# Adapters in fp16 halves, turned by DMA, in a four-layer conditioned residual kernel

## The reference

```
x = x + attention16(x, f)                 # 16 heads of 32; K, V from x and f, Q from f; @ Wo + bo
x = x + softmax((x + embed[stage]) @ f.T) @ f
x = x + layernorm(x + relu(x @ W1 + b1) @ W2 + b2) * gamma + beta      # W1: 512x128, by language
x = x + (x @ lora_A.T) @ lora_B.T + lang_embed                         # rank 16, by language
```

## Time and profile before

| what | value |
|---|---|
| median of 3 runs | 1295.74 us (1295.46 to 1296.12) |
| the profiled execution | 1295.73 us, span 1294.0 us |
| busy: PE, PEld | 1257.0 us (97%), 523.5 us (40%) |
| busy: DVE, ACT, POOL | 864.2 us (67%), 847.8 us (66%), 490.0 us (38%) |
| mean granted PE clock | 0.991 |

### The profile page before, as it was taken

How to read it: one execution, slowest core, us unless ns; L and a number is a source line. 1 busy time by engine, 2 the same in 40 slices (tenths; PEclk the granted TensorE clock), 3 DMA queues, 4 the chain that set the end, 5 groups by cost and what they waited for, 6 DMA issues and landing times.

```text
span 1294.0 us, 19231 instructions
## 1 busy us (share of the span) xinstructions
PE 1257.0 (97%) x6697; PEld 523.5 (40%) x6697; DVE 864.2 (67%) x1561; ACT 847.8 (66%) x1795; POOL 490.0 (38%) x428
## 2 busy tenths in 40 slices
PE   7999999999999999999999999999999999999996
PEld 4332454325543354433544245442454324543243
DVE  6886459764697538975389743987449855597544
ACT  5887359863598536975379742888339873598631
POOL 6604353233631246331552416514344143532024
PEclk9999999999999999999999999999999999999996
DMA  6303522225224153142421333213432136222020
GB/s 217 83 6 107 124 57 66 79 80 99 52 63 122 37 98 68 47 125 63 86 58 50 117 79 77 58 50 108 98 75 66 46 95 124 50 66 90 4 33 33
DMA packets 156142, 98.85 MB, mean 76 GB/s; under 512 B 107338, under 2 KB 130182, under 8 KB 156046
## 3 DMA queue, kind: packets, MB, share of 16 engines
q1 hardware_dynamic: 155984, 97.61, 30.9%
q10 hardware_dynamic: 62, 0.01, 0.0%
HBM read 40.81 MB, written 8.40 MB: 38 GB/s over the span
## 4 chain that ended last, share of the span: by engine, by line
PE 69%; DVE 15%; ACT 12%; issue 2%; POOL 1%; DMA 1%; SPq 0%; ACTq 0%; POOLq 0%; DVEq 0%
PE bank L478 25%; PE banks L478 13%; PE banks L1443 8%; DVE nmx L1095 8%; PE bank L1459 7%; ACT banks L816 5%; PE banks L1378 4%; ACT big L867 4%; PE bank L1280 3%; PE bank L1406 2%; PE bank L1411 2%; PE bank L1433 2%; PE bank L1469 1%; DVE y L1053 1%; ACT bank L896 1%
## 5 line engine op out<-in xcount | busy, mean ns | idle before, releaser
L816 ACT ACTIVATE banks<-banks,nmx 128x512 f32<-128x512 f32 x512 | 341.2, 682 | 40.2 <-DVE nmx L1095 37.8
L1095 DVE TENSOR_REDUCE nmx<-banks 128x1 f32<-128x512 f32 x512 | 329.2, 687 | 19.5 <-PE banks L1378 18.6
L867 ACT ACTIVATE big<-banks 128x1024 f32<-128x1024 f32 x256 | 248.0, 1021 | 54.4 <-PE banks L1443 53.4
L478 PE MATMUL bank<-fT,w_hi 128*128 128x512 f16 x768 | 255.7, 379 | 0.6 <-DVE fT L1009 0.6
L1378 PE MATMUL banks<-KQ 97*128 97x512 f16 x512 | 195.6, 382 | 8.1 <-ACT banks L816 7.9
L513 POOL TENSOR_TENSOR split<-tiles_in,ones 128x512 f16<-128x512 f32 x56 | 62.0, 1108 | 224.7 <-DMA xT<-split 205.7
L1443 PE MATMUL banks<-KQ 98*128 98x512 f16 x512 | 143.5, 383 | 3.6 <-DVE q L1116 0.2
L478 PE MATMUL bank<-fT,w_lo 128*128 128x512 f16 x384 | 145.4, 379 | 0.0
L513 POOL TENSOR_TENSOR half<-qk,ones 128x512 f16<-128x512 f32 x64 | 68.4, 1069 | 200.6 <-ACT qk L798 192.5
L1459 PE MATMUL bank<-big,V 128*32 128x512 f32 x1024 | 136.4, 605 | 0.0
L588 POOL TENSOR_TENSOR x<-x,bo_rows 128x512 f32<-128x512 f32 x32 | 39.9, 1275 | 206.5 <-DMA x<-in_x_dram 206.5
(11 more groups left out here) (154 smaller groups left out, 1822.0 us busy)
## 6 DMA issues: line engine op xcount, KB each, us to landing
KQ<-half SPq DMA_DIRECT2D x384, 64.0 KB, 2.0
tiles_in<-in_x_dram SPq DMA_DIRECT2D x32, 256.0 KB, 7.7
x<-in_x_dram SPq DMA_DIRECT2D x8, 1024.0 KB, 5.7
out_dram<-x SPq DMA_DIRECT2D x32, 256.0 KB, 2.0
tiles_in<-in_fside_BxSxS_dram SPq DMA_DIRECT2D x28, 256.0 KB, 3.8
w<-in_L_cond_W_dram SPq DMA_DIRECT2D x16, 256.0 KB, 4.5
b2r<-in_L_cond_b_dram SPq DMA_DIRECT2D x8, 256.0 KB, 4.3
gr<-in_L_cond_gamma_dram SPq DMA_DIRECT2D x8, 256.0 KB, 5.5
```

Of the source, the lines that this page charges most:

```text
L478: mm = eng.matmul(out_ap, pairs[n][0], pairs[n][1], start=(first and n == 0), stop=(last and n == len(pairs) - 1))
L816: eng.activation(bank(step, i)[:, v, :], bank(step, i)[:, v, :], ACT.Exp, bias=nmx[:, t, h:h + 1], accum_out=esum[:, t, h:h + 1]).then_inc ...
L867: eng.activation(big[:, n % 2, 2 * u:2 * u + 2, :], bank(step)[:, :, :], ACT.Exp).then_inc(read(step), 1)
L1095: eng.tensor_reduce(nmx[:, t, h:h + 1], bank(step, i)[:, v, :], AX_X, ALU.max, negate=True).then_inc(max_done, 1)
```

## The change

In all batches but the last the adapters' turns leave PE. `X2` (at the head of the middle stage) splits x into an fp16 high half (ACT) and a low half (VectorE, right behind each PV1 addition) in p16, and SP turns each tile by DMA into aT2. `X3` splits the normed x on GpSimd, and `T3` has SP turn it. In the last batch PE still turns, and high and low halves are taken by ACT and VectorE behind it. w1, lora_A and lora_B are held as fp16 halves: HID is made by `hi_lo` with 256 columns for two tiles at once, LOW by 16 f16 matmuls of 256 columns, LORA by one f16 matmul a tile. ADP stays fp32. The norm is rewritten: `U` takes (y - mean) * gamma on VectorE before the root is known, Newton is 11 operations of fused form over all four tiles (over two in the last batch), and SCALE is one VectorE operation. The addition of beta is moved ahead. The list of the middle stage is new, and SP turns tile 0 of f earlier.

```diff
+        at = {3: [("HID", 0)], 5: [("ADP", 0)], 6: [("ADP", 1), ("SQ", 0)], 7: [("HID", 1), ("SQ", 1)], 8: [("U", 0)],
+              9: [("ADP", 2), ("U", 1)], 10: [("ADP", 3), ("SQ", 2)], 11: [("SQ", 3), ("U", 2)], 12: [("NORM", 0), ("U", 3)],
+              13: [("SCALE", 0), ("SCALE", 1)], 14: [("X3", 0), ("SCALE", 2), ("SCALE", 3)], 15: [("X3", 1)],
+              16: [("X3", 2), ("T3", 0)], 17: [("X3", 3), ("T3", 1)], 19: [("T3", 2)], 20: [("T3", 3)],
+              24: [("LOW", 0)], 25: [("LORA", 0)], 27: [("LORA", 1)], 29: [("LOW", 1)], 31: [("LORA", 2)], 33: [("LORA", 3)]}
+        adapters = [at.get(n, []) for n in range(max(at) + 1)]
...
+    out, later = [("X2", t) for t in range(NT) if tail], {}
...
# GpSimd
+                    elif step[0] in ("X2", "X2T"):
...
+                        eng.tensor_tensor(yb[:, t, :], x1[:, t, :], b2r[:, :], ALU.add).then_inc(xb_done, 1)
+                        if head and t == NT - 1:
+                            add_beta(range(NT), head, i)
...
+                    elif step[0] == "X3":
                         t = step[1]
-                        eng.wait_ge(normed, i * NT + t + 1)
-                        eng.tensor_tensor(y[:, t % 2, :], y[:, t % 2, :], gr[:, :], ALU.mult).then_inc(scaled, 1)
-                        eng.wait_ge(scaled, i * NT + t + 1)
-                        eng.wait_ge(xg_done, i * NT + t + 1)
-                        eng.tensor_tensor(x1[:, t, :], y[:, t % 2, :], x1[:, t, :], ALU.add).then_inc(x3_done, 1)
+                        eng.wait_ge(x3_done, i * NT + t + 1)
+                        eng.wait_ge(x2t_in[t // 2], i * 32 + 32)
+                        split(p16[:, t, 0:S], p16[:, t, S:2 * S], x1[:, t, :], x3_hi, i * NT + t + 1, x3_lo)
# SP
+                    elif step[0] == "T3":
+                        t = step[1]
+                        eng.wait_ge(x3_lo, i * NT + t + 1)
+                        turn(aT2, t, p16[:, t, :], x3t_in[t // 2])
...
                 for t in range(NT):
+                    if head and t == NT - 1:
+                        wait_full(eng, ("S1", NT - 1), i)
+                        turn_f(0, b)
                     wait_read(eng, ("S1", t), i)
                     eng.dma_start_transpose(p1T[:, t, :, :, :].rearrange("p h k n -> p (h k) n"), p16[:, t, :]
                                             ).then_inc(p1t_in[t], 16)
                 if head:
-                    for n in range(NT):
-                        eng.wait_ge(f_lo, b * NT + n + 1)
-                        turn(fT, n, b, ft_in)
+                    turn_f(1, b)
+                    for t in range(NT):
+                        if t == NT // 2:
+                            turn_f(2, b)
+                            turn_f(3, b)
+                        eng.wait_ge(x2_lo, i * NT + t + 1)
+                        turn(aT2, t, p16[:, t, :], x2t_in[t // 2])
# VectorE
+            def norms_of(n, head, i):
+                tiles = NT if head else NT // 2
...
+                eng.wait_ge(sq_done, i * NT + at.stop)
+                eng.tensor_scalar(var, st[:, at, 2], 1.0 / D, EPS, ALU.mult, ALU.add).then_inc(newton, 1)
+                eng.wait_ge(newton, base + 1)
+                eng.tensor_scalar(r_int, si[:, at, 3], -0.5, 0x5F3759DF, ALU.mult, ALU.add).then_inc(newton, 1)
+                for k in range(base + 2, base + NEWTON, 3):
+                    eng.wait_ge(newton, k)
+                    eng.scalar_tensor_tensor(out=c, in0=var, scalar=-0.5, in1=r, op0=ALU.mult, op1=ALU.mult).then_inc(newton, 1)
...
+            def centre(t, i):
+                eng.wait_ge(sq_done, i * NT + t + 1)
+                eng.scalar_tensor_tensor(out=yb[:, t, :], in0=yb[:, t, :], scalar=st[:, t, 1:2], in1=gr[:, :],
+                                         op0=ALU.add, op1=ALU.mult).then_inc(normed, 1)
+            def scale(t, head, i):
...
+                eng.scalar_tensor_tensor(out=x1[:, t, :], in0=yb[:, t, :], scalar=st[:, t, 4:5], in1=x1[:, t, :],
+                                         op0=ALU.mult, op1=ALU.add).then_inc(x3_done, 1)
...
+                        if head:
+                            eng.wait_ge(x2_hi, i * NT + t + 1)
+                            eng.scalar_tensor_tensor(out=p16[:, t, S:2 * S], in0=x1[:, t, :], scalar=1.0, in1=p16[:, t, 0:S],
+                                                     op0=ALU.mult, op1=ALU.subtract).then_inc(x2_lo, 1)
# PE
                     elif kind == "LOW":
+                        at = tokens(step, head)
+                        if head:
+                            eng.wait_ge(x3t_in[step[1]], i * 32 + 32)
...
+                        for d in range(ND):
+                            for h in range(2):
+                                rows = a16[:, h, d, :, :].rearrange("p c r -> p (c r)")
+                                mm = eng.matmul(bank(step, i)[0:3 * LR, 0:at.stop - at.start], rows, aT2[:, h, d, at],
+                                                start=(d == h == 0), stop=(d == ND - 1 and h == 1))
```

More of the change, by code:

```diff
@@ L122, in order_mid @@
         if adapters and i % 2 == 0:
-            out += [a for a in (adapters.pop(0),) if a]
+            out += adapters.pop(0)
         if rows and not sums and i >= late and not adapters:
@@ L134, in order_mid @@
     assert rows and i >= max(later)
-    return out + [a for a in adapters if a] + ([] if sums else [("SROW",)])
+    return out + [a for each in adapters for a in each] + ([] if sums else [("SROW",)])
 OPEN = ((32, 26, 26, 26), (24, 24, 24, 24))
@@ L210, in order_last, with tokens @@
             + [("X2T", 0), ("HID", 0), ("X2T", 1), ("PV1", 2), ("ADP", 0), ("HID", 1), ("SQ", 0),
[L211 to L214, removed]
+               ("PV1", 3), ("ADP", 1), ("U", 0), ("SQ", 1), ("X2T", 2), ("U", 1), ("NORM", 0),
+               ("HID", 2), ("X2T", 3), ("SCALE", 0), ("HID", 3), ("X3T", 0), ("SCALE", 1), ("ADP", 2), ("LOW", 0),
+               ("X3T", 1), ("SQ", 2), ("ADP", 3), ("LOW", 1), ("U", 2), ("SQ", 3), ("U", 3), ("NORM", 1),
+               ("LORA", 0), ("LORA", 1), ("SCALE", 2), ("X3T", 2), ("SCALE", 3), ("LOW", 2), ("X3T", 3),
                ("LORA", 2), ("LOW", 3), ("LORA", 3)])
-ADAPTER_STEPS = set(order_mid(True, False))
+ADAPTERS = ("X2", "X2T", "HID", "ADP", "SQ", "U", "NORM", "SCALE", "X3", "T3", "X3T", "LOW", "LORA")
+def tokens(step, head):
+    n = NT // 2 if head else 1
+    return slice(step[1] * n * P, (step[1] + 1) * n * P)
 def plan_banks():
@@ L598, in _ @@
             add_bo(B - 1)
[L599 removed]
+            split_w1(B - 1)
+            mid(True, False, B - 1, [step for step in order_last() if step[0] in ADAPTERS])
         @block.sync
@@ L870, in attention @@
                 wait_full(eng, ("PREPB",), i)
[L871 to L873 removed]
+                eng.activation(lowB[0:LOW_ROWS, :], lone[2][0:LOW_ROWS, :], ACT.Copy, scale=WS).then_inc(b_hi, 1)
             def layer1(i, head, order=ORDER_L1):
@@ L1197, in attention @@
                     take_norms(g, i)
-                for g in range(1, NG):
+                finish_group(1, i)
+                small_columns(i)
+                for g in range(2, NG):
                     finish_group(g, i)
+                eng.wait_ge(b_hi, i + 1)
+                low = slice(2 * LR, 3 * LR)
+                eng.scalar_tensor_tensor(out=lowB[low, :], in0=lone[2][low, :], scalar=WS, in1=lowB[low, :],
+                                         op0=ALU.mult, op1=ALU.subtract).then_inc(read(("PREPB",)), 1)
             def layer1(i, head, order=ORDER_L1):
@@ L1480, in small_tables @@
                 mm.then_inc(done(("PREPB",)), 1)
-                eng.transpose(lone[3][:, 0:NT], erow[:, :], ident[0:NT, 0:NT])
-                for d in range(ND):
-                    mm = eng.transpose(lone[3][:, NT + d * LR:NT + (d + 1) * LR],
-                                       small[:, d * P:(d + 1) * P], ident[0:LR, 0:LR])
-                mm.then_inc(done(("PREPA",)), 1)
             def attention(i):
```

324 lines of the change are left out of this document (180 added, 144 removed).

## The result

The changed kernel takes 1364.47 us (median of 4, 1362.30 to 1367.83) against 1295.85 us for the kernel before: ratio 1.0532, 95% interval 1.0510 to 1.0554, 68.6 us slower. The forecast was slower by 20 us. All of the loss lies in the seven middle stages (batches 0 to 6), which take 96.4, 96.9, 93.0, 95.1, 96.8, 94.0 and 94.1 us, 95.2 us in the mean, where each took 85.5 us: 7 x 9.7 = 68 us. The last batch, from its first attention matmul to the end of the span, takes 109.4 us against 110.4 us. Every stage is from the one execution that was profiled, at 1362.3 us the shortest of the four.

What follows compares the result with a forecast made beforehand. The matmul engine PE, busy 97% of the span, was taken as the bound. 1295.7 + 23.1 (seven middle stages) − 2.5 (last batch) = 1316 us, own range 1298 to 1338, 8-in-10 range 1284 to 1348.

Steps and rivals of the forecast that it cites:

- What PE gives up: Adapters in the seven batches before the last: PE work falls from 15.4 to 8.6 us, saving 6.8 us a batch.
- First wait, at Q 0: Middle stage: PE waits at Q 0 for DMA turns of fT, 2.0 us a batch, bounds 1.1 to 2.9.
- What GpSimd does to VectorE: VectorE operations on two SBUF operands starting beside a GpSimd pass end with it: 0.99 to 1.01 us against 0.16 alone.
- Second wait: At LOW 0 for DMA turns of x3: chain 25.3 us against 15.8 us of PE work, wait 9.5 us.
- Middle stage 88.8 us: Sum of PE steps, two waits and gaps: 88.8 us against 85.5 us, +3.3 us a batch, seven times +23 us.
- rival Three: PE's standing in middle stages also costs its clock, 3.5 us a batch, 1340 us; chance 0.14.
- small gaps: Middle stage: 3.4 us between counted PE steps and measured time before; 2.0 us kept after, bounds 1.0 to 3.0.
- Rival One: At LOW 0: turns land in time, chain under 15.8 us, PE stays the bound, 1245 us; chance 0.14.
- Costed at nothing: Attention's extra VectorE work, some 2 us, its W1 split on GpSimd, 3.4 us, and PREPA and PREPB turns add nothing.
- The last batch, -2.5 us: Tail, turns kept on PE: shorter Newton and norm against later low halves, -5.8 us at best, nothing at worst, -2.5 taken.
- Two: Middle stage: both waits at their low ends, 84.0 us, tail 2.5 to 5 us shorter, about 1286 us; chance 0.12.
- What would show it: Middle-stage signs: PE stands before LOW 0 and at Q 0, stage 86 to 92 us; wrong if clock falls below 1.00.

Runs made afterwards that it cites:

- both: Changed kernel with SyncE's turns of f put ahead of x2 and LOW 0 and the five steps behind it six places later: 1310.80 us, ratio 1.0103.

## Why the prediction was right in direction and wrong in size

**What PE gives up, 6.8 us a batch.** Right: PE is busy 77.4 us in the last window and 84.7 us in that of before. In after and in "both" it is spent on waits.

**First wait, at Q 0: 2.0 us forecast.** It is 2.7 us in batch 1 and 14.1 us over seven stages, 2.0 us in the mean; without it 15.1 us come back.

**What GpSimd does to VectorE.** Two Newton operations held, 0.91 and 1.02 us, as forecast. The Trainium skill, page GPSIMD Engine Reference, section Key points, says that the two engines contend where an instruction of VectorE has two SBUF inputs or is in a 2-port perf mode. For two inputs the trace of after agrees (1.02 against 0.17 us).

**Second wait, chain of 25.3 us from ADP 3 to LOW 0.** 25.4 us, from 348.11, where the slot behind ADP 3 starts, to 373.49. The parts: to the start of X3 0 7.1 us (5.6 + 1.7 forecast), GpSimd 5.7 us (4.5, and some of the 2.0 for collisions), SP 7.7 and 1.4 us, landing 3.4 us. The wait was forecast at 9.5 us, partly at SMAX; it is 3.2 + 4.2 = 7.4 us, and the rest is PE's own steps, 18.0 us in place of 15.8 us, with up to 1.7 us of it lost to the half clock.

**Middle stage 88.8 us, and this is the step that failed.** Measured 95.2 us in the mean, 96.9 in batch 1. The forecast's sum "30.9 + 2.0 + 9.5 + 44.4 + 2.0" gives 42.4 us up to LOW 0, where batch 1 took 45.8, and 46.4 us behind it, where it took 51.1. Two things are missing, and they are where the sum failed. One is the clock, which the sum put at nothing: rival Three, "PE's standing also costs its clock", held a chance of 0.14 and 3.5 us a batch and was no term of the sum. It came in every middle stage, and taking it away gave back 2.5 us a batch. The Trainium skill, page TensorE: Matmul & The Clock Gate, section HAM oscillation, says that a matmul engine that waits long enough for a DMA starts its next work cold. The trace of after agrees at both DMA waits of batch 1 (2.7 and 4.2 us), and the same happened at its wait for ScalarE (3.2 us), though not in every stage.

The other is the term for small gaps, "of these I keep 2.0 us, since VectorE and ACT have less to do there". Its reason does not hold for VectorE, which is busy 68.4 us in the stage against 64.1 us before (ScalarE 60.1 against 62.6). And it was reasoned the wrong way round: with less on PE, more of each round trip of matmul, maximum and exponential is bare. Behind LOW 0 batch 1 holds 3.0 us of waits at banks that ScalarE gives back, where before had 0.8 us in the whole stage, and 2.1 us of half clock. Repaired of both large DMA waits, a stage still holds 8.7 us of waits, 3.2 us of them at the fifth SMAX, which the sum had inside its second wait. Rival One even named it ("ACT would then be close behind", 50.6 beside 47.9 us), and yet took all 48 us as gained. Of the 6.4 us a batch by which the stage was under-sized, at least 2.5 us are the clock, shown by the filled waits. That the remaining 3.9 us are mostly waits of the ring is in keeping with the 3.5 us a stage that short exponentials return in after; no run separates the two parts exactly, since a shorter wait also changes the clock.

**Costed at nothing.** Right: attention 34.8 to 35.4 us and L1 35.4 to 36.4 us against 35.2 and 35.4.

**The last batch, -2.5 us.** Measured -1.0. The operations fell away as counted, but PE now stands for low halves (`DVE big L1208`), and one of these waits in VectorE's queue behind eleven Newton operations, the last of them held:

```profile
1332.98 1.24 DVE L1094 SCALAR_TENSOR_TENSOR st<-st 128x2 f32<-128x2 f32 x1
1334.14 0.68 DVE L1208 TENSOR_TENSOR big<-bank,big 128x512 f16<-128x512 f32 x1
```

**Rivals.** One needed the chain under 15.8 us; it took 25.4. Two needed both waits at their low ends, gaps of 1.0 us and a full clock; the first wait was in the middle of its bounds and the stage 11 us longer than its 84.0 us. Its own terms give 1280 to 1283 us and not 1286, and the low ends of the forecast's own bounds give about 1286 us, where its range begins at 1298; neither bears on the miss. Three was right in kind and too small in time (1340 us).

**What would show it.** The waits stood where it said, and LOW 0 started 25 us behind ADP 3. It called itself wrong if the granted clock fell below 1.00 in the middle stages: it fell to 0.93 in batch 1. The stage, 86 to 92 us by the forecast, took 93.0 to 96.9 us.

No version that computes all of the result beats the kernel before. Left open is whether an order of VectorE's work exists that keeps both the maxima and the adapters on time, and whether the stand at the fifth SMAX can be removed without paying it elsewhere.

## What to carry to other kernels

Where the busiest engine is at 99% of a stretch and two others at 92 and 94%, taking work from the first is worth only what these two leave; test that cheaply by shortening the second engine's operations before moving any work of the first. A wait put into a stream of matmuls can be priced twice, once as standing and once as the half clock that comes with it: in batch 1 10.1 us of standing at three places, and 2.5 us of clock in the mean, stood against 6.8 us saved. A DMA on a queue that is worked off in order waits for what stands ahead of it: twelve small ones were 7.7 of the 25.4 us.

## What the runs showed of the hardware

- Three stands of 2.7, 3.2 and 4.2 us in one stage each came with a stretch at 0.50, of 3.4, 3.4 and 6.8 us, though the clock had been 1.00 for 23.9 us between the first two.
- The length of a stand did not settle it. In "both", six stages have the same stand of 3.2 us at the fifth SMAX; four of them fell to 0.50 for 3.4 or 6.8 us and two stayed at 1.00.
- Useless matmuls in the waits made the program 17.8 us faster.
- A VectorE operation with one SBUF input, 128x4, took 0.17 us in after and 1.23 us beside GpSimd's additions of two tensors. The forecast had expected holds for two inputs only. The trace of before had one too: the TENSOR_SCALAR on L1046 took 0.17 us alone and 1.19 us at 335.59, beside GpSimd's addition of b2 (L550).
- Full passes of VectorE took longer beside GpSimd too. SCALE took 1164 ns in the mean against some 740 for one alone, and U 0 beside a half on GpSimd 1.30 us:

```profile
L1106 DVE SCALAR_TENSOR_TENSOR x<-tiles_in,st,x 128x512 f32<-128x512 f32 x4 | 4.4, 1164 | 0.0
```

- An exponential with a sum over 128 columns takes 342 ns where 512 columns take 673 ns, and the read of its accumulator 195 ns against 217 to 233 ns: a quarter of the columns is half of the time.
